# A graph network kernel: one more target tile gathered by edge, one fewer summed through masks

## The reference, cut to what matters

```python
for l in range(L):                       # 2 layers
    xb = h.reshape(N, B, S)              # 8 blocks of 12 channels
    transformed = jnp.einsum('nbi,rbio->rnbo', xb, weights[l]).reshape(R, N, D)   # 8 relations
    msg = transformed[etype, src] * edge_norm
    agg = jax.ops.segment_sum(msg, dst, num_segments=N)
    h_new = agg + h @ loop_w[l] + bias[l]
    h = jax.nn.relu(h_new) if l < L - 1 else h_new
```

## Time and profile before

| | |
|---|---|
| median of 3 runs | 2478.81 us (2478.54 to 2480.23) |
| the profiled execution | 2479.42 us |
| its span, first to last instruction | 2477.7 us |
| mean granted TensorE clock | 0.956 |
| first relational layer, mask tiles and groups | from 1578 to 1913 us of the span |
| second relational layer, the same part | from 1967 to 2302 us |

### The profile page before, as it was taken

One profiled execution on the slowest core, in us unless ns is written; L12 is line 12 of the kernel. 1 busy time (PEld: TensorE's weight loads), 2 busy tenths in 40 slices (PEclk: granted clock), 3 DMA queues, 4 the chain that ended last, 5 costly groups with the idle time before them and its releaser, 6 DMA issues. The chain is left out here.

```text
span 2477.7 us, 64255 instructions
## 1 busy us (share of the span) xinstructions
PE 2143.1 (86%) x22305; PEld 1794.2 (72%) x22306; DVE 1959.9 (79%) x2888; ACT 1282.1 (52%) x2996; POOL 595.8 (24%) x879
## 2 busy tenths in 40 slices
PE   2888887899999998677776776999999999999897
PEld 2777777899999997212121112799999599999787
DVE  8889989655565664799999997798887688888446
ACT  1888888333333333699999995533221623221323
POOL 3444443000000000200000000355554255555000
PEclk8999999999999999899999997999999999999799
DMA  2344444100010100511111113332232522232710
GB/s 67 146 166 170 169 162 159 69 29 28 28 41 29 41 15 19 134 41 41 42 42 42 41 43 113 141 85 81 78 85 46 195 76 79 79 86 45 296 45 21
DMA packets 94264, 205.31 MB, mean 83 GB/s; under 512 B 21204, under 2 KB 60756, under 8 KB 93952
## 3 DMA queue, kind: packets, MB, share of 16 engines
q1 hardware_dynamic: 80384, 182.39, 21.2%
q0 software_dynamic: 13696, 20.25, 4.2%
HBM read 116.99 MB, written 84.76 MB: 81 GB/s over the span
## 5 line engine op out<-in xcount | busy, mean ns | idle before, releaser
L1875 PE MATMUL l_bank<-tab,mask 128*128 128x192 f16 x7600 | 636.2, 247 | 6.9 <-PEq L1526 3.5
L1875 PEld LDWEIGHTS l_bank<-tab,mask 128*128 128x128 f16 x7600 | 630.2, 98 | 8.5 <-issue 8.1
L1461 DVE TENSOR_SCALAR mask<-code 128x1600 int32<-128x1600 int32 x304 | 548.6, 1817 | 87.2 <-PE l_bank L1875 86.3
L1851 POOL DMA_INDIRECT ggot<-table_dram,gidx x408 | 385.6, 945 | 263.2 <-PE l_bank L1875 255.5
L1342 DVE SCALAR_TENSOR_TENSOR pr<-ex,cring 128x1568 f32<-128x1568 f32 x200 | 356.5, 1783 | 10.3 <-DMA cring<-c_dram 10.3
L1288 PE MATMUL att_acc<-pr,v 128*32 128x392 f32 x1600 | 187.0, 541 | 141.6 <-DVE pr L1342 132.0
L891 PE MATMUL sums<-onehots,ct 128*128 128x192 f16 x3125 | 264.4, 248 | 11.8 <-issue 7.6
L891 PEld LDWEIGHTS sums<-onehots,ct 128*128 128x128 f16 x3125 | 261.6, 99 | 14.6 <-issue 8.1
L891 PE MATMUL sums<-u,ct 128*128 128x192 f16 x3125 | 259.1, 246 | 0.0
L891 PEld LDWEIGHTS sums<-u,ct 128*128 128x128 f16 x3125 | 258.0, 98 | 0.0
L1316 ACT ACTIVATE ex<-score_rest,poss 128x1176 f32<-128x1176 f32 x200 | 250.0, 1250 | 4.2 <-PE score_rest L1280 4.2
(11 more groups left out here) (349 smaller groups left out, 3149.8 us busy)
## 6 DMA issues: line engine op xcount, KB each, us to landing
code<-code_dram SPq DMA_DIRECT2D x38, 800.0 KB, 4.5
code_dram<-flat SPq DMA_DIRECT2D x100, 200.0 KB, 1.9
ct_dram<-ct SPq DMA_DIRECT2D x25, 800.0 KB, 3.5
c_dram<-flat SPq DMA_DIRECT2D x25, 800.0 KB, 3.4
ct_again<-ct_dram SPq DMA_DIRECT2D x25, 800.0 KB, 17.8
cring<-c_dram SPq DMA_DIRECT2D x200, 98.0 KB, 1.9
table_dram<-tab SPq DMA_DIRECT2D x50, 384.0 KB, 2.3
flat<-code_dram SPq DMA_DIRECT2D x19, 800.0 KB, 4.4
```

The lines of the kernel that those rows point to most:

```text
L1461: e.tensor_scalar(turned.rearrange("p (s q d) -> p s q d", q=NQ, d=DQ // 2), words.rearrange("p (q s d) -> p s q d", q=NQ, d=DQ // 2), abs ...
L1851: e.indirect_dma_start(ggot[:, k, j, :], None, table_dram[:, :], bass.IndirectOffsetOnAxis(ap=gidx[:, k, j:j + 1], axis=0)).then_inc(s_ggo ...
L1875: mm = e.matmul(acc[k][:, 0:2 * D], mask[:, r % MR, s, :], tab[:, s, r, :], start=(r == 0 and s == 0), stop=(r == R - 1 and s == NT - 1))
```

## The change

GT goes from 6 to 7. Tile 18 is gathered, and 18 tiles are left to the masks. Everything else follows by the formulas: 20 groups and 240 gathers a layer, ticks spread over 3600 matmuls in place of 3800, and another tile behind which each group's products stand. `oh`, `node`, the check of counts and the loop over irregular edges cover 18 tiles.

```diff
-GT = 6
+GT = 7
 TD = NT - GT
 GG = 12
 SLOTS = 3
```

## The result

The changed kernel takes **2581.38 us** (median of 4 runs, 2580.01 to 2582.67) against 2479.24 of the kernel before: 4.1% slower, ratio 1.041 (95% interval 1.0394 to 1.0425). The forecast was 2452, 1.1% faster, with 0.03 on slower.

The account below looks back on a forecast made before the run. PE was taken to bound the relational layers: -27.3 us of its work plus 2 x 0.2 of end wait gave -26.9, from 2479.42 to 2452.5, and with the runs' median 0.6 lower, 2452 us; range 2450.5 to 2457.

Parts of the forecast that it names:

- 0.03 on slower: Whole kernel: the chance given to a slowdown of more than 5 us, beside 0.95 on faster and 0.02 within it.
- POOL, the pace: Relational layers: ticks 1.216 us apart against POOL's own pitch of 1.25; lag between 0 and 1 us.
- PE's units: Relational layers, from PE's timeline: 16.50 us per mask tile of 200 matmuls, 0.99 us per group of 12 products.
- POOL sets the end: Rival, layer's end: mean gather pitch beyond 1.367 us makes the kernel slower, 2504 us at 1.42; chance 0.03.
- three signs of being wrong: Mid-layer: PE waiting for DMA ahead of groups, gathers lasting over 1.0 us, or masks slower than 1.82 us.
- what would be seen: New profile: tile period 16.50, groups 0.99, gather pitch 1.22 to 1.25, end gap at most 1 us.
- -13.63 us a layer: PE's work in a relational layer: -16.50 for a mask tile, +2.97 for three groups, -0.10 for irregular edges.
- the last group's landing: Layer's end, group (6,2): gathers land 2.5 us after issue, PE waits 0.2 us a layer; 2.3 at 5.0.
- pick-up: Layer's end: POOL's delay after ACT's gather indices for the last group are ready, taken as 0.4 us.
- forecast gain of 26.9: Whole kernel: -27.3 us of PE work in both layers plus 2 x 0.2 us of end wait.
- landings are late: Rival, gathers: landings of 5.0 us cost +5.6 in all, giving 2457 to 2458 us; chance 0.13.

Follow-up runs that it names:

- kernel a: Changed kernel (GT=7) with node and oh allocated for 19 tiles, so later buffers keep their old places: 2457.66 us against 2476.44 for the kernel before.
- s: Changed kernel with each gather fetching 64 of its 128 rows, same number of ticks and gathers: 2586.45 us against 2481.41 for the kernel before.
- m: The program of kernel a, unaltered, on another chip: 2581.60 us against 2483.31 for the kernel before.
- f: Changed kernel with node alone allocated for 19 tiles, moving later buffers: 2569.0 us against 2477.72 for the kernel before.
- g: Changed kernel with oh alone allocated for 19 tiles, moving later buffers: 2565.3 us against 2477.72 for the kernel before.
- h: Changed kernel with only the gathered groups' buffers at its places, 768 bytes lower, zero and what follows at old ones: 2567.1 us against 2477.72 before.
- j: Changed kernel at old places except buffers from base to goh, 256 bytes lower: 2579.3 us against 2480.47 for the kernel before.
- k: Changed kernel at old places except buffers from base to goh, and ggot, 256 bytes lower: 2580.6 us against 2480.47 for the kernel before.
- q: Kernel before (GT=6) with twice the PE ticks, POOL waiting for every second, gathers as before: 2480.58 us against 2481.41.
- r: Changed kernel with one PE tick for every three gathers: 2586.35 us against 2481.41 for the kernel before.
- kernel o: Kernel before (GT=6), old places, with ticks 14.73 matmuls apart: 2578.86 us (profiled execution) against 2483.31.

## Why the prediction was wrong

**The step that failed** is the one under "POOL, the pace". It costed the denser gathers by what they do to POOL: duration, pitch, lag, landing. It then let PE's units of the earlier trace rows stand: 16.50 us a tile at any pace. On three of the chips here and in the run of the result PE loses 0.14 to 0.26 us for each gather issued at ticks 1.32 to 1.22 us apart. The size agrees with the result. Without stalls the two layers would be 2 x 321.6 us (326.45 of kernel a's first layer less its one wait of 4.83); they were 386.0 + 383.7, so 126.5 more. Busy and idle time of the mask matmuls are 716.4 us where kernel a has 610.9, 105.5 of it; the rest lies at the groups' products and the irregular part, ahead of which PE stood for 9.7 and 3.9 us in the same way; some 7 us of it no row names.

**The evidence that misled.** The prediction had "the first 11 gathers ran at 1.25 pitch" against late landings, and never asked what that pitch does to PE. Rows 5 seemed to answer it: PE's first 200 matmuls stand there in one row without a pause. On chip D three such gathers are enough to make PE stand. The trace of before shows no stall there, as the traces from chip A don't; whether it comes from such a chip no record says. One profile could not have shown this effect.

**No rival named it.** "POOL sets the end" had the sign but not the mechanism: gathers kept a median of 944 ns and PE never waited for POOL at the end. None of its three signs of being wrong came up either: PE never waits for a DMA in mid-layer, and gathers and masks keep their durations. What failed was on its list of what would be seen, PE's tile period of 16.50: 18 tiles and 20 groups took 386.0 us, 20.3 us a tile when each group is given its 0.99. The chance of 0.03 on slower was too small for a change that takes a rate beyond what any long stretch of the trace shows.

**What was right**, seen where PE wasn't held up, on chip A. PE's timeline of kernel a:

```profile
1734.75 16.66 PE L1875 MATMUL l_bank<-tab,mask 128*128 128x192 f16 x200
1751.25 2.14 PE L1883 MATMUL l_bank<-ggot,goh 128*128 128x192 f16 x24
1753.23 16.66 PE L1875 MATMUL l_bank<-tab,mask 128*128 128x192 f16 x200
1769.73 1.15 PE L1883 MATMUL l_bank<-ggot,goh 128*128 128x192 f16 x12
```

16.50 and 0.99 are there, two groups behind tiles 2, 9 and 17, and 321.6 us for the layer without waits where 321 was forecast. The units, the count of groups and the -13.63 us a layer hold. Masks stayed at a median of 1820 ns in the changed kernel as well.

**What was mis-sized even there: the last group's landing.** The forecast took 0.2 us a layer, from a landing of 2.5, and kept 2.3 for one of 5.0. In kernel a, timeline of the end of the first layer:

```profile
1876.05 0.21 ACT L1935 ACTIVATE gidx<-rowidx 128x12 int32 x1 [29.43 <-PE l_bank L1883]
...
1877.03 0.94 POOL L1851 DMA_INDIRECT ggot<-table_dram,gidx  x1 [4.90 <-PE l_bank L1875]
...
1890.78 0.94 POOL L1851 DMA_INDIRECT ggot<-table_dram,gidx  x1 [0.30 <-issue]
...
1892.16 1.15 PE L1883 MATMUL l_bank<-ggot,goh 128*128 128x192 f16 x12
...
1898.14 1.66 PE L1883 MATMUL l_bank<-ggot,goh 128*128 128x192 f16 x12 [4.83 <-DMA ggot<-table_dram,gidx]
```

POOL's eleven pitches are 13.75 us, as worked out; its pick-up took 1877.03 - (1876.05 + 0.21) = 0.77 us where 0.4 was taken. The landing wasn't a constant. Of the gathers from 1876, from 1880, from 1884 and from 1888 it was:

```profile
DMA to landing us min/median/max: 2.4/2.6/3.5
...
DMA to landing us min/median/max: 3.5/4.2/4.9
...
DMA to landing us min/median/max: 4.9/6.0/6.7
...
DMA to landing us min/median/max: 7.0/7.2/7.3
```

So the wait was 4.8 us in the first layer and 4.7 in the second, 9.6 in both where 0.4 was taken: 9.2 of the forecast gain of 26.9, which leaves 17.7, and 18.8 was measured. That is the rival "landings are late", with twice the wait that it priced and neither by code loads nor by the pitch alone. In mid-layer of the same kernel eight gathers, five of which waited for no tick, landed in 2.4 to 3.4 us, and the DMA engines were busy for 0.17 of the time; at the end they are busy for 0.88 and move less:

```profile
DMA to landing us min/median/max: 2.4/2.5/3.4
...
1840.00:1850.00 10.00, 10.00 (x124) 10.00 (x122) 8.49 (x7) 5.60 (x15) 6.89 (x8) 1.00 0.17 37
1884.00:1894.00 10.00, 9.31 (x113) 9.08 (x111) 2.16 (x2) 0.00 (x0) 5.90 (x7) 1.00 0.88 31
```

What differs is what they fetch. 103,125 edges fill 806 chunks; the row indices are filled up with 0 to 816 (`memset`, line 1433), so the last ten gathers of each layer fetch row 0 of the table 128 times each. The first two of (6,2), at 1877.03 and 1878.28, landed after 2.6 and 2.4 us; the ten behind them after 3.5 to 7.3, one every (1890.78 + 7.3 - 1879.53 - 3.5) / 9 = 1.67 us. Their packets took 0.57 to 1.64 us on average over a gather, where those of the others took 0.22 at the median. The last ten stand out so in both layers of every run with whole gathers, the kernel before included (0.56 to 1.01 us there in the first layer); in s, with 64 rows in each, they don't. A fill with different rows was not tried. In the changed kernel itself this wait is hidden, since PE comes so much later: (6,0) and (6,2) run back to back in both layers:

```profile
1962.15 2.14 PE L1883 MATMUL l_bank<-ggot,goh 128*128 128x192 f16 x24
...
2400.73 2.23 PE L1883 MATMUL l_bank<-ggot,goh 128*128 128x192 f16 x24
```

**What stays open.** Why PE's rises are held when gathers come often, and why not on chip A, isn't settled. PE's stalls carry no releaser, the granted clock stays at 1.00, and excluded by runs are the buffers' places (a against m; f, g, h, j, k), PE's ticks (q, r) and the rows and bytes moved (s). A backlog in the gathers' queue is no likely cause: on chip A landings stay at 2.5 us at the median in mid-layer, and half-size gathers didn't help on D. A run in which POOL pauses of itself after every second or third gather, at the same mean rate, would test the reading of the order of events above; there is none. Whether a few gathers in a row or their mean rate is what counts was not separated: late ticks release several gathers at once, so on B, C and D the one brings the other. Chip A was used in one job only, so "chip" may also mean what else was going on then.

No version here beats the kernel before on all chips. Kernel a (2457.66) does on A, by 0.7%, and loses 98 us on D; GT=6 with its ticks 1.51 us apart is the one that never lost.

## What to carry to other kernels

An indirect gather from POOL isn't free for the other engines just because POOL has time: past a certain rate (here between one in 1.51 and one in 1.32 us) it can cost PE 0.14 to 0.26 us each. Before more work is moved to such DMAs, raise their rate alone, with the work unchanged (kernel o, one line), and read the row of the engine that must not be disturbed. Look at what filled-up indices fetch: behind ten gathers of one and the same row PE waited 4.8 us in a layer of kernel a. When experiments from different jobs are compared, repeat one kernel that lost and one that didn't side by side before a theory is built: here eight kernels went into a theory of places that one pair in one job overturned.

## What the runs showed of the hardware that was not expected

- PE stands for 0.2 to 1.1 us between matmuls with no releaser in the profile, and goes on when POOL has paused and PE's semaphore rises come through (38 of 44 times in 280 us of the changed kernel). At times it runs one to three matmuls at a time, about 0.72 us apart (changed kernel, end of the first layer):

```profile
1947.74 0.24 PE L1875 MATMUL l_bank<-tab,mask 128*128 128x192 f16 x1 [0.30 <-issue]
1948.47 0.41 PE L1875 MATMUL l_bank<-tab,mask 128*128 128x192 f16 x3 [0.49 <-issue]
1949.19 0.24 PE L1875 MATMUL l_bank<-tab,mask 128*128 128x192 f16 x1 [0.32 <-issue]
1949.91 0.33 PE L1875 MATMUL l_bank<-tab,mask 128*128 128x192 f16 x2 [0.48 <-issue]
```

- PE's semaphore updates, 0.26 us after the matmul's start in the kernel before, come up to 5.5 us after it in the changed one.
- The same program differs by 5.0% between chips (2457.66 and 2581.60), while the kernel before differs by 0.3% (2476.44 to 2483.31).
- Gathers whose 128 indices all name one row land only every 1.67 us when they are issued every 1.25, so that the tenth lands 7.3 us after its issue; gathers of different rows at that pitch landed in 2.4 to 3.4 us in mid-layer (kernel a). A gather of 64 rows still occupies POOL for 898 ns at the median, against 944.
